# Self attention's opening slots laid between the last eight tiles of the routed layer before it

## The reference, cut to what matters

```python
x = x + tanh(g_ffn[2]) * _L2_ffn_ref(_layernorm(x), ...)      # 8 experts, 2 chosen per token
x = x + tanh(g_xattn[3]) * _L3_xattn_ref(_layernorm(x), cond, ...)

# _L2_ffn_ref: for each token and each of its two experts
out = linear[e] @ (gelu(x @ gate[e]) * (x @ up[e]))           # hidden width 256, weighted sum of the two

# _L3_xattn_ref
ln_out = _ln(hidden_states)                                   # a second norm, with weights
q, k, v = (fp8_linear(ln_out, w) for w in (wq, wk, wv))       # inputs rounded to fp8 values
core = gqa(_ln(q), _ln(k), v)                                 # self attention, 16 heads, 8 key heads
xout = gqa(_ln(fp8_linear(ln_out, wqx)), _ln(kx), vx)         # cross attention, kx and vx from cond
out = fp8_round(concat(core, xout)) @ wproj
```

## Time and profile before

| | |
|---|---|
| median of 3 runs | 1362.86 us (1362.01 to 1368.53) |
| profiled execution | 1366.97 us, of which the span is 1365.2 us |
| PE busy | 1260.6 us (92%) |
| DVE busy | 965.3 us (71%) |
| ACT busy | 815.7 us (60%) |
| POOL busy | 669.8 us (49%) |
| DMA | 159.62 MB, mean 117 GB/s |
| PE in the routed layer's tiles | 616.7 to 721.7 us |
| first scores of layer 3's attention | 753.7 us |

### The profile page before, as it was taken

How to read it: one execution, slowest core, us unless ns; L and a number is a source line. 1 busy time by engine, 2 the same in 40 slices (tenths; PEclk the granted TensorE clock), 3 DMA queues, 4 the chain that set the end, 5 groups by cost and what they waited for, 6 DMA issues and landing times.

```text
span 1365.2 us, 23538 instructions
## 1 busy us (share of the span) xinstructions
PE 1260.6 (92%) x7122; PEld 1056.4 (77%) x7122; DVE 965.3 (71%) x2457; ACT 815.7 (60%) x2057; POOL 669.8 (49%) x720
## 2 busy tenths in 40 slices
PE   6999999998799999989897699999999999999994
PEld 3556888886588888878784578888887888888784
DVE  7997555776787778734654677877778787877753
ACT  6954222333676767745543587677777777776353
POOL 1112555542343434542432475657768776765453
PEclk9999999998999999998999799999999999999998
DMA  6223555362232223335644980001320110032383
GB/s 235 85 101 120 163 174 175 114 188 72 85 109 72 81 71 110 121 148 182 227 158 154 317 270 1 1 1 32 108 71 32 39 56 32 32 119 107 102 302 110
DMA packets 90139, 159.62 MB, mean 117 GB/s; under 512 B 9324, under 2 KB 50953, under 8 KB 89515
## 3 DMA queue, kind: packets, MB, share of 16 engines
q1 hardware_dynamic: 82811, 144.55, 32.0%
q0 software_dynamic: 6640, 12.67, 2.8%
q10 hardware_dynamic: 576, 1.05, 0.2%
HBM read 103.86 MB, written 58.17 MB: 119 GB/s over the span
## 4 chain that ended last, share of the span: by engine, by line
PE 66%; DVE 12%; issue 7%; ACT 5%; POOL 4%; DMA 4%; SPq 0%; POOLq 0%; ACTq 0%; DVEq 0%
PE ps L1612 9%; PE ps L1744 9%; PE ps L1717 8%; PE ps L1695 7%; PE ps L1762 6%; PE ps L1626 5%; PE ps L1727 5%; PE ps L1880 4%; PE ps L1706 3%; PE ps L1445 3%; POOL urs L1152 2%; DMA rows_out<-tile_y,tile_to 2%; PE ps L1891 2%; DVE usum L3241 1%; ACT probs L2463 1%
## 5 line engine op out<-in xcount | busy, mean ns | idle before, releaser
L1159 POOL TENSOR_TENSOR probs<-probs,prec 128x512 f32<-128x512 f32 x192 | 202.3, 1054 | 281.7 <-DVE prec L3277 281.6
L2463 ACT ACTIVATE probs<-ps,nmax 128x256 f32<-128x256 f32 x384 | 178.8, 472 | 186.8 <-DVE nmax L3270 120.9
L1717 PE MATMUL ps<-k_feat,q_feat 128*128 128x256 f32 x768 | 199.4, 382 | 2.7 <-ACT q_feat L2453 1.9
L1744 PE MATMUL ps<-probs_t,v_tok 128*128 128x256 f32 x768 | 197.7, 380 | 0.2 <-ACT ob L2482 0.2
L1152 POOL TENSOR_TENSOR urs<-uve,neg_half 128x4 f32<-128x4 f32 x136 | 137.0, 1008 | 59.4 <-DVE uve L3242 48.5
L1717 PEld LDWEIGHTS ps<-k_feat,q_feat 128*128 128x128 f32 x768 | 137.2, 191 | 16.7 <-issue 3.5
L1744 PEld LDWEIGHTS ps<-probs_t,v_tok 128*128 128x128 f32 x768 | 130.9, 190 | 10.4 <-ACT probs_t L2472 0.4
L1727 PE MATMUL ps<-ident,probs 128*128 128x128 f32 x768 | 116.3, 274 | 16.0 <-ACT probs_t L2472 14.9
L1727 PEld LDWEIGHTS ps<-ident,probs 128*128 128x128 f32 x768 | 92.4, 140 | 48.8 <-issue 21.7
L2472 ACT ACTIVATE probs_t<-ps 128x512 f32<-128x512 f32 x192 | 115.4, 601 | 2.1 <-PE ps L1727 2.1
L2382 ACT ACTIVATE gated<-ps 128x512 f32<-128x512 f32 x48 | 28.7, 598 | 135.6 <-PE ps L1612 135.6
(11 more groups left out here) (489 smaller groups left out, 3429.2 us busy)
## 6 DMA issues: line engine op xcount, KB each, us to landing
rows_in<-zero_rows SPq DMA_DIRECT2D x3, 5200.0 KB, 33.9
mid_more_w<-in_l2f_w SPq DMA_DIRECT2D x14, 768.0 KB, 4.5
tile_w<-in_l3f_w SPq DMA_DIRECT2D x21, 385.5 KB, 6.6
mid_rows<-mid_zero SPq DMA_DIRECT2D x6, 1040.0 KB, 5.5
w<-in_l1f_w SPq DMA_DIRECT2D x24, 256.0 KB, 4.8
spread_w<-we_dram SPq DMA_DIRECT2D x16, 384.0 KB, 3.6
mid_w<-in_l2f_w SPq DMA_DIRECT2D x8, 768.0 KB, 5.8
kv_cross<-kv_out SPq DMA_DIRECT2D x20, 256.0 KB, 2.0
```

Source lines behind the costliest of these rows:

```text
L1159: pool.tensor_tensor(p3, p3, spread(prec[g % 3][:, :], [P, TB, S]), ALU.mult)\
L1717: mm = pe.matmul(ps[g % 2][:, j * S:(j + 1) * S], q_feat[:, h, j * P:(j + 1) * P], k_feat[:, kv, :], start=True, stop=True)
L1744: mm = pe.matmul(ps[6][:, 0:S], v_tok[:, tb, kv * P:(kv + 1) * P], probs_t[g % 2][:, tb, :], start=tb == 0, stop=tb == TB - 1)
L2463: ins = act_e.activation(probs[g % 4][:, j, :], ps[g % 2][:, j * S:(j + 1) * S], ACT.Exp, bias=nmax[g % 3][:, j:j + 1], **kw, accum_out=ps ...
```

## The change

On PE, ACT, DVE and POOL the generator of layer 3's attention is made before the loop over tiles, and the loop takes steps of it: after tile j's own work PE takes slot j - 31 for j = 23 to 31, ACT slot j - 32 for j = 24 to 32, DVE slot j - 31 for j = 23 to 29, and POOL slot j - 28 for j = 20 to 28. So slots -8 to 0 (on DVE -8 to -2) lie between tiles. What this takes with it:

- the banks: rows are turned into bank 0 alone and down projections go to bank 6 alone; the opening's projections go to banks 1, 7, 4, 1 and then 2 and 3; the keys of cross attention to 7 and 4;
- batches 1 and 2 are added, normed, turned and copied two to five tiles earlier; batches 3 and 4 are added at t = 3 and 4 rather than 0 and 1, and normed, turned and copied one to three slots later;
- the eight pieces of keys move to slots -2 to 1, and SP stores four of them before it waits for the last puts;
- output weights are split at t = 5, 8, 11, 14 on ACT and t = 6 to 16 on POOL;
- a fifth buffer for later weights, and SP's order around it;
- the first eight row loads are issued before SP waits for the end of layer 2's mixes; the weights of expert 7 come after that wait, those of expert 2 with experts 4 to 6.

```diff
-        return 4 + p if self.fp8 and p in (2, 3) else 2 + p % 2
+        return (1, 7, 4, 1)[p] if self.fp8 and p < 4 else 2 + p % 2
...
-KV_LATE_AT = ((-6, -4, -3), (-6, -5, -5, -4, -4, -3))
-KV_LATE_FIRST = (1, 2)
+KV_LATE_AT = ((-6, -4, -3), (-2, -1, -1, 0, 0, 0, 1, 1))
+KV_LATE_FIRST = 1
+MID_SLOTS = (23, 32)
...
-MID_SETS = 4
+MID_SETS = 5
...
 # SP
                 sp.wait_ge(*mid_at("placed", 16 * CHOICES * half))
-                sp.wait_ge(s["o_ready"], L2X.total)
                 for j in range(MID_RING):
                     rows(j)
+                sp.wait_ge(s["o_ready"], L2X.total)
+                sp.dma_start(mid_w[7][:, :], T["l2f_w"][7]).then_inc(mid_signal("w_in7"), 16)
...
                 sp.wait_ge(*mid_at("placed", 16 * CHOICES * NT))
-                for j in range(first_b, first_b + 4):
+                for j in range(first_b, first_b + 5):
                     rows(j)
-                later(MID_SETS + 2)
-                rows(first_b + 4)
                 more = registers(1)
-                for i in range(4):
-                    later(MID_SETS + 3 + i)
+                for i in range(5):
+                    later(MID_SETS + 2 + i)
                     rows(first_b + 5 + i)
...
+                first_kv = len(KV_ALL) - KV_GAPS[2]
+                store_kv(first_kv, first_kv + 4, kv_late)
                 for i in range(4):
                     sp.wait_ge(*mid_put_all(MID_ALL, i))
...
 # POOL
-                if t in (1, 2, 112, 113, 127):
+                if t in (4, 5, 112, 113, 127):
                     part_scales(1)
-                if 3 <= t < 11:
-                    i = t - 3
+                if 6 <= t < 17 and t % 3 < 2:
+                    i = (t - 6) // 3 * 2 + t % 3
                     low = low_output(wsets[1]["o"], slice(2 * i, 2 * i + 2), i // 2 + 1)
...
-                if j in (20, 21):
+                if j in (17, 18):
                     part_scales(1)
+                if MID_SLOTS[0] <= j + 3 < MID_SLOTS[1]:
+                    next(l3x)
...
 # PE
-                if j >= 2:
-                    pe.wait_ge(*mid_at("copied", j - 1))
+                if j:
+                    pe.wait_ge(*mid_at("copied", j))      # mid_turn, now always bank 0
...
-                if j >= 2:
-                    pe.wait_ge(*mid_at("out", j - 1))
+                if j:
+                    pe.wait_ge(*mid_at("out", j))         # mid_down, now always bank 6
...
-                if j in (26, 27):
-                    b = j - 26
+                if j in (22, 23):
+                    b = j - 22
                     turn_part(LAST_LN, b, h_late, quantised, (LAST_LN - 1) * B + b + 1, ps[4 + b])
                 if j >= 2:
                     mid_down(j - 2)
-            pe.wait_ge(*mid_at("out", MID_ALL))
-            keys_values(KV_LATE_FIRST[1], ps[0:2])
+                if j == 25:
+                    pe.wait_ge(part_out, LAST_LN * B + 2)
+                if j >= MID_ALL - 1:
+                    pe.wait_ge(*mid_at("act", min(j, MID_ALL)))
+                if MID_SLOTS[0] <= j < MID_SLOTS[1]:
+                    next(l3x)
...
 # ACT
-                if j in (25, 26):
-                    centre_part(LAST_LN, j - 25, h_late)
-                if j in (28, 29):
-                    copy_late(LAST_LN, j - 28)
+                if j in (22, 23):
+                    centre_part(LAST_LN, j - 22, h_late)
+                if j in (23, 24):
+                    copy_late(LAST_LN, j - 23)
+                if MID_SLOTS[0] < j <= MID_SLOTS[1]:
+                    next(l3x)
...
 # DVE
-                if j in (21, 22):
-                    mid_add(j - 21)
-                    part_moments(LAST_LN, j - 21)
-                if j in (23, 24):
-                    part_shift(LAST_LN, j - 23)
+                if j in (20, 21):
+                    part_shift(LAST_LN, j - 20)
+                if j in (19, 20):
+                    mid_add(j - 19)
+                    part_moments(LAST_LN, j - 19)
+                if MID_SLOTS[0] <= j:
+                    next(l3x)
...
-                if t in (0, 1):
-                    mid_add(2 + t)
-                    part_moments(LAST_LN, 2 + t)
+                if t in (3, 4):
+                    mid_add(t - 1)
+                    part_moments(LAST_LN, t - 1)
```

More of the change, by code:

```diff
@@ L1280, in beside_l2x @@
                     mid_scatter(2)
-            run(attention(L2X, beside_l2x))
-            part_scales(1)
-            root_mean_square(2)
-            for j in range(MID_ALL):
-                pool.wait_ge(*mid_at("out", j + 1))
-                pool.indirect_dma_start(mid_out[:, :], bass.IndirectOffsetOnAxis(ap=mid_to[:, j:j + 1], axis=0),
-                                        mid_y[j % 4][:, :], None, bounds_check=CHOICES * NTOK - 1,
-                                        oob_is_err=False).then_inc(mid_signal(f"put{j % 4}"), 16)
-                if j in (4, 7):
-                    pool.wait_ge(*mid_at("places", 3 + (j - 4) // 3))
-                if j in (4, 5, 7, 8):
-                    mid_scatter(2)
-                if j in (20, 21):
-                    part_scales(1)
             def last_low_first(i):
@@ L1370, in scatter @@
                                             h_near[:, t, :], None).then_inc(placed, 16)
-            run(attention(L3X, low_cross))
+            run(attention(L2X, beside_l2x))
+            l3x = attention(L3X, low_cross)
+            part_scales(1)
+            root_mean_square(2)
+            for j in range(MID_ALL):
+                pool.wait_ge(*mid_at("out", j + 1))
+                pool.indirect_dma_start(mid_out[:, :], bass.IndirectOffsetOnAxis(ap=mid_to[:, j:j + 1], axis=0),
+                                        mid_y[j % 4][:, :], None, bounds_check=CHOICES * NTOK - 1,
+                                        oob_is_err=False).then_inc(mid_signal(f"put{j % 4}"), 16)
+                if j in (4, 7):
+                    pool.wait_ge(*mid_at("places", 3 + (j - 4) // 3))
+                if j in (4, 5, 7, 8):
+                    mid_scatter(2)
+                if j in (17, 18):
+                    part_scales(1)
+                if MID_SLOTS[0] <= j + 3 < MID_SLOTS[1]:
+                    next(l3x)
+            run(l3x)
             pool.wait_ge(zeroed, 16 * 4)
@@ L1884, in mid_down @@
-            def mid_down(j):
-                pe.wait_ge(*mid_at("act", j + 1))
-                if j >= 2:
-                    pe.wait_ge(*mid_at("out", j - 1))
-                w = mid_weights(j)[:, MID_GU:MID_W].rearrange("p (k d) -> p k d", k=2)
-                for fb in range(2):
-                    mm = pe.matmul(ps[6 + j % 2][:, 0:D], mid_act[:, j % 3, fb * P:(fb + 1) * P], w[:, fb, :],
-                                   start=fb == 0, stop=fb == 1)
-                mm.then_inc(mid_signal("down"), 1)
@@ L2009, in toward_l3f, with mid_turn, mid_gates @@
                     last_gates(0)
-            run(attention(L3X, toward_l3f))
+            def mid_turn(j):
+                pe.wait_ge(*mid_rows_loaded(j))
+                if j:
+                    pe.wait_ge(*mid_at("copied", j))
+                for kb in range(KB):
+                    mm = pe.transpose(ps[0][:, kb * P:(kb + 1) * P], mid_x[j % MID_RING][:, kb * P:(kb + 1) * P],
+                                      ident[:, :])
+                mm.then_inc(mid_signal("turned"), 1)
+            def mid_gates(j):
+                pe.wait_ge(*mid_at("copied", j + 1))
+                pe.wait_ge(*mid_weights_loaded(j))
+                if j >= 2:
+                    pe.wait_ge(*mid_at("act", j - 1))
+                w = mid_weights(j)[:, 0:MID_GU].rearrange("p (k g f) -> p k g f", k=KB, g=2)
+                for g in range(2):
+                    for fb in range(2):
+                        for kb in range(KB):
+                            at_ = (2 * g + fb) * P
+                            mm = pe.matmul(ps[2 + j % 2][:, at_:at_ + P], w[:, kb, g, fb * P:(fb + 1) * P],
+                                           mid_feat[j % 2][:, kb, :], start=kb == 0, stop=kb == KB - 1)
+                mm.then_inc(mid_signal("gates"), 1)
@@ new lines, in mid_down @@
+            def mid_down(j):
+                pe.wait_ge(*mid_at("act", j + 1))
+                if j:
+                    pe.wait_ge(*mid_at("out", j))
+                w = mid_weights(j)[:, MID_GU:MID_W].rearrange("p (k d) -> p k d", k=2)
+                for fb in range(2):
+                    mm = pe.matmul(ps[6][:, 0:D], mid_act[:, j % 3, fb * P:(fb + 1) * P], w[:, fb, :],
+                                   start=fb == 0, stop=fb == 1)
+                mm.then_inc(mid_signal("down"), 1)
```

232 lines of the change are left out of this document (110 added, 122 removed).

## The result

The changed kernel takes 1356.24 us, the median of six runs (1352.45 to 1357.79 and one of 6031, which the ratio and the interval leave out; 1355.69 without it), against 1365.15 for six runs of the kernel before: a ratio of 0.9926, 95% interval 0.9906 to 0.9945. Run again beside later kernels it took 1353.90 (1351.07 to 1356.16) against 1365.57, ratio 0.9905 (0.9884 to 0.9926); of that second measurement I had expected 1354 to 1357 us. It is faster by 9 to 12 us, where 21.9 were forecast; the first median lies above the range of 1332 to 1354, the second at its edge. The direction was right, the size wrong. The profiled execution took 1355.69 us, span 1353.9.

The account below looks back on a forecast made before the run. The seam into layer 3's attention was taken as latency-bound. Terms -5.6 + 1.9 - 18.2 - 7.2 + 5.5 = -23.6 took the profiled 1366.97 to 1343.4, median 1339.3; moved by 1.7, the forecast was 1341.0, range 1332 to 1354.

Parts of the forecast that it names:

- Part 4: Slots -8 to 0 beside tiles 23 to 29: turn of tile 24 to scores of slot 1 in 44.0, not 62.15: -18.2.
- Part 3: Earlier norms of batches 1 and 2: results land at 684 to 686, DVE waits 1 to 3 us: +1.9.
- Part 1: Early rows: first rows still wait for the last scatter, so nothing starts earlier: 0.
- Part 2: Fifth weight set: turn 15 to turn 16 loses its wait for weights, rows landing in time: -5.6.
- Part 5: Slots 1 to 3: 9.5 us instead of 16.7, without two additions and the clock's loss: -7.2.
- Part 6: What comes back later: additions of batches 3 and 4 at t = 3, 4 (+4.5), POOL's low parts (+1): +5.5.
- The rule against it: DVE's rounding steps beside POOL's puts block each other on a shared port pair: some 0.6 us in all, within bounds.
- rival (a): Half given back: DVE becomes the bound from part 3 on; gain 11.6, time 1351; chance 0.24.
- (b): Only the weight set counts, as late results of batches 1 and 2 hold tiles: -5.6, time 1357; chance 0.09.
- (c): Slower: a tile's and a unit's chains run one behind the other, 11.6 us a slot: 1399.7; chance 0.05.
- signs of being wrong: PE's holes between tiles 23 and 29 over 10 us, batch 1's results after 690, or slot 12 after 795.

Follow-up runs that it names:

- E2: Changed kernel with slots -8 to 0 run after tile 29 instead of beside tiles 23 to 29, five weight sets kept: 1363.57 us, ratio to before 0.9983.
- E1: Changed kernel with slots -8 to 0 run after tile 29 and four later weight sets instead of five: 1373.12 us, ratio to before 1.0051.
- E4: Changed kernel with four key pieces of slots 0 and 1 moved to slots 3 to 6, batch 4's late norm one slot later: 1349.38 us.
- E8: Changed kernel with matmuls nobody reads put in PE's holes of slots 0 and 1: 1351.89 us, ratio to before 0.9893.
- after again: The changed kernel itself, measured a second time beside later kernels: 1353.90 us, ratio to before 0.9905.
- E3: Changed kernel with first results' loads issued ahead of rows of tiles 25 and 26, and three later weight loads behind them: 1349.84 us.
- E6: E5 with three more key pieces moved between scores and projections of slots 0 to 2, two of their stores behind batches 3 and 4's results: 1341.24 us.
- E5: Changed kernel with both E3's order in SP's queue and E4's four key pieces at slots 3 to 6: 1348.93 us.
- E7: E5 with GpSimd's low parts of output weights spread over slots 6 to 19, and ScalarE's high parts at 5, 8, 12, 16: 1349.47 us.
- E9: E6 with the key piece left at slot -2 moved between the two turns of slot 2: 1342.48 us, ratio to before 0.9817.
- E10: Changed kernel with later weights of tiles 25 to 27 loaded behind the first results, whose issue stays behind those rows: 1350.93 us.

## Why the prediction was wrong

The direction and the mechanism held: slots laid between tiles fill PE (35.98 of 38.10 us), and E2 shows that this brings the gain. What failed is the size, in two steps above all: the price of the last slot without a tile (part 4) and the wait for the first results (part 3).

**Part 1 (0):** right. The rows were issued at 616.54, the last scatter having landed at 616.47.

**Part 2 (-5.6):** right in number, 5.56 from turn 15 to turn 16 in the profile, and 5.8 from turn 13. That "the rows next to it land in time" was not: the wait for the rows of tile 15 came up from under the weights. It cost 1.8 us ahead of turn 15 in this profile, which the vanished wait ahead of turn 14 happened to pay back. In other traces with five sets it was up to 3.8 us, with slow matmuls behind it, so that from turn 13 to turn 16 between 10.7 and 15.0 us went by and the gain was 1.4 to 5.8.

**Part 3 (+1.9):** 5.4 in the profile after (turn 16 to turn 24: 28.34 for 22.97). Of that 3.0 is the one wait ahead of tile 22's gates, 0.4 the turn, and some 1.9 the lower clock behind the wait, for which the forecast had nothing. The step that failed is "landing 4.2 to 6.5 later, so 684 to 686": they landed at 688.7. This trace ran 1.7 behind the forecast's turn 16, so the miss itself is smaller: 19.7 us behind turn 16, where 16.6 to 18.6 were forecast. Of it 0.5 is the issue, which now waits for the write of tile 14's result, and the landing took 6.9. I took the landing from the earlier trace rows and did not count that the fifth buffer releases five weight loads within 5.3 us where they had been spread over 14.8, all just ahead of the writes that the results wait for. That is not the whole cause: in E1, whose loads are spread as before, DVE still waits 2.7 us. In the other traces of the same order part 3 costs 6.5 (E2: 29.51) and 1.3 to 2.5 (E4, E8, after again: 24.28, 24.58, 25.49). These are not independent of part 2. In all five the results land 18.2 to 19.1 us after the first of the five weight loads leaves, and where tile 15's rows held PE longer, less was left to wait for. Tiles together (parts 2 and 3) were to shrink by 3.7; from turn 15 they shrank by 0.2 and 1.7, from turn 13 by 0.4 and nothing. With SP's queue mended they shrank, from turn 13, by 5.4 and 5.3 in E3 and E6, and by 1.1 to 3.2 in E5, E7 and E9, which waited longer for tile 15's rows.

**Part 4 (-18.2)** is the step that failed most: 62.15 became 49.26, -12.9. The slots beside the tiles are not where it failed: the scores of slot 0 stand 38.1 us after the turn of tile 24, where I had said about 37. The other 4.2 is slot 0 itself, 11.17 us for about 7, with three key pieces, a hole and the lower clock in it. Three terms. The key pieces: I priced six at 1.31, from the step from one to the next instruction; two pieces in a row step 3.44, so one is 1.72, and the missing 0.41 stood in the slow first projection behind it (0.80). That is 2.5. The clock, which the forecast had at 1.0 all through: 1.5 to 1.8 (E1, E8). And the waits, 3.5 in all (1.33, 1.38, and two of 0.4 for ACT), against 3.0 allowed. The remaining 0.5 to 0.8 I can't place. PE's busy time in the stretch is 45.8 us where I had 41.0. One window of the kernel before would have warned me, since the busy time less two pieces (3.4) is 47.2:

```profile
695.93:758.08 62.15, 50.60 (x257) 36.59 (x256) 28.86 (x90) 27.03 (x56) 17.01 (x20) 0.97 0.46 160
```

**Part 5 (-7.2):** -4.8. The two pieces of slot 1 are 3.44 and not 2.6, and the waits of 1.38 and 1.71 are what a unit's chain leaves when nothing stands beside it: 11.89 for 9.5.

**Part 6 (+5.5):** slots 3 to 12 as told (39.4 us, the additions at 761.03 and 767.94); slots 12 to 16 cost 1.6 and those after them 0.9, instead of 1: 6.9 in all.

**The rule against it:** nothing came of it. From 698 to 736 us the puts took 0.97 to 1.10 us, and the first rounding step 0.61 to 0.69 (0.61 to 0.81 before).

Together: 3.5 + 5.3 + 2.4 + 1.4 = 12.6 against the 12.3 us by which the profiled time missed 1343.4 (the small rest is drift: the trace after ran 2.0 behind before the change begins, and gained 2.1 behind slot 31).

The rival (a), half given back, was nearer in all: a gain of 11.6 (8.9 and 11.7 measured), with part 3 at +4 (5.4), part 4 at -13 (-12.9), part 5 at -4 (-4.8) and part 6 at +7 (6.9). Its reason was wrong: DVE was the bound only in slots 3 to 6. So it is luck that its terms fit. (b) and (c) are out: no slot beside a tile's gates took more than 4.6 us (from one tile's gates to the next). Of the signs of being wrong one came, slot 12 at 798.0, later than 795; the results of batch 1 landed before 690, and PE had under 1 us of holes between tiles 23 and 29.

What the forecast got wrong in kind: I walked the queues and allowed for the holes of slots 0 to 2, but left the movable work (the key pieces) on top of them instead of asking where it would be free. E6 and E9 put it there and reach, in the seam, 19.3 and 21.2 us for the forecast 19.9, though with other code than the forecast was for.

## What to carry to other kernels

Where two stages are laid side by side, the last slots, which have nothing beside them, are the price: keep independent work of the size of a hole (here 1.7 us for holes of 1.4) for the middle of these slots, between the instruction that starts a latency chain and the one that waits for it, not for their ends. A load that became free to go early goes with all that became free with it; order a queue by who is waited for, and when removing one wait brings nothing in a trace, look for a second one that ends at the same time. And price an instruction from two equal ones in a row, then check the sum against the busy time of the window.

## What the runs showed of the hardware

- The granted clock fell in some executions and not in others of the same code with the same holes: 0.78, 0.92 and 0.89 in E5, 1.00 in all three stretches of E7, worth 4.3 us. In slot 0, in the seven traces with the code of the kernel after, it was 0.85 five times, 0.73 in E10 and 1.00 in E1.
- The indirect write of tile 14's result landed 5.47 us after its start with the DMA engines at a share of 1.02 in that time (after, 676.26 to 681.73), and within 3.2 at a share of 0.40 (E3, 675.26 to 678.49).
- DVE's tensor_scalar on four sums (uve, 128x4) took 0.53 us beside GpSimd's multiplication of the probabilities (752.72 and 758.53 in the trace after), and 0.17 in slot 0 (741.21, 742.91), when GpSimd was idle. The Trainium skill (SBUF — State Buffer, "Who interferes with whom") has the two engines take one port pair in turns for some DVE operations, of which tensor_scalar can be one; this trace agrees in direction, as the earlier trace rows did.
